# Window attention stage: token products over the whole array in three fp32r passes, staged in a ring and placed by transfers

## Chip, core and metric

The kernel runs on one core of one Trainium2 chip. TensorE (PE) does the matmuls, PEld is its weight load, VectorE is DVE, ScalarE is ACT, GpSimd is POOL, and SyncE (SP) issues every DMA of this kernel. The metric is the device time in microseconds (us) of one execution, the median of several.

## What is computed

Four residual blocks follow each other on x of 16 sequences x 256 tokens x 128 channels. The change lies in the last, which takes more than two thirds of the time. Cut to what matters:

```python
for i in range(6):                                   # DEPTH layers
    x = attn_layer(shift_tokens(x), Wqkv[i], ...) + x
    x = ffn_layer(shift_tokens(x), ...) + x
# attn_layer: 16 heads of 64, windows of 32 tokens; each looks at itself and the one before
q, k, v = split(x @ Wqkv)
q, k = l2norm(q) * qs, l2norm(k) * ksc, then rotary
attn = softmax(where(mask, -max, q @ k.T * 8))       # 32 x 64 per window and head
out = (attn @ v) in head order, then out @ Wo
```

The kernel never forms v. Since out @ Wo is a sum over heads of attn @ (x @ Wv_h @ Wo_h), it first makes one 128x128 matrix M_h = Wv_h Wo_h for each head (once in a layer) and then U_h = x @ M_h for each sequence. U is what this text calls the token products: 256 tokens x 16 heads x 128 channels.

## The kernel before, in words

The last stage (phase D) runs 6 layers x 16 sequences = 96 units, in 100 turns. Turn f works on several units at once: it projects q and k for unit f (chunks 0 to 4) and f-1 (chunks 5 to 7), takes the softmax of f-2 and makes its token products, runs attention for f-3 and the feed-forward of f-4. Each engine has an order written out by hand (the loops `for f in range(TURNS_D)`), and waits on semaphores. Nothing is reordered at run time, so an instruction that waits holds all behind it on its engine, SP's DMAs included.

Names. `project(n, i)` is 6 fp32r matmuls (a high and a low part of weights and tokens; three products of the parts) into bank 0 or 1; ACT squares the bank (`squares`), DVE multiplies it with the rotary table (`rotary_products`, L1428) into one of three slots `d_t`, and POOL adds halves (`rotary_sums`, L1815, into `d_rot`; `add_halves`, L1823). `norm_*`, `spread_norms` and `scale_keys` (L1464) apply the norms. `place_queries` (L2141) and `place_keys` (L2132) are 8 DMAs each on SP that bring `d_rot` into the layout of `d_q` and `d_k`; the first waits for POOL's eighth rotary sum, the second for DVE's second `scale_keys`. `scores` waits for both; so does POOL's first rotary sum of the next unit, which overwrites what `place_keys` reads. POOL's softmax steps are `scale_shifted` (L1832) and `softmax_scale` (L1838); ACT's is `softmax_exp` (L1676), DVE's are L1470, L1476, L1483 and the transposes L1496.

`token_products(n, w)` (L1957) makes U for window w of 8: plain fp32, and since a window has 32 tokens, four column groups of the array work side by side, one for each four heads. Its result has the 32 tokens of a window on 32 partitions and heads by groups of four down the 128, which is the layout in which `attention` reads `d_u`; ACT's `read_products` (L1684) copies each bank there. Windows use banks 5 and 4 in the order 5, 4, 5, 4, 5, 5, 4, 5; window w waits until an earlier one has left its bank. `attention(n, 0)` waits for the first windows' copies and `attention(n, 1)` for all. `head_matrices` makes the M_h in turn 16 l + 2 of layer l.

Of the kernel before, what the change touches and what calls it, by code (L numbers as in the profile page):

```python
# [67 lines left out]
LOADS_A, LOADS_B, LOADS_C, LOADS_CONST, CONSTS = 3, 4, 5, 10, 7  # L68
# [3 lines left out]
def build(nc, dram, out):  # L72
    ctx = ExitStack()
    with ctx:
# [14 lines left out]
        ones_row = sb("ones_row", [1, P])  # L89
# [5 lines left out]
        sel_r = sb("sel_r", [P, 4, 2, P], F32R)  # L95
        odd = sb("odd", [P, 1])
        z_split = sb("z_split", [P, 2, T], F32R)
        m_vo = sb("m_vo", [P, H, C])
        wvt = sb("wvt", [P, PAIRS, C])
        wo = sb("wo", [P, PAIRS, C])  # L100
        wqk_stage = sb("wqk_stage", [P, 2 * INNER])
        wqk_split = sb("wqk_split", [P, 8, 2, 2, P], F32R)
        x_split = sb("x_split", [P, 2, 2, T], F32R)
# [6 lines left out]
        ARENA = 30300  # L110
# [10 lines left out]
        parts_r = under_arena("parts_b", PARTS_B_AT, 2 * 4 * P * (1 + 2 * HB))  # L121
        WEIGHTS_C = 3 * PAIRS * C
        PARTS_C_AT = (4 * PAIRS + 1) * C + 3 * NT + TPS * C
        low_weights_c = under_arena("weights_c_low", C, WEIGHTS_C)
        parts_c = under_arena("parts_c", PARTS_C_AT, 4 * TPS * P + WEIGHTS_C)
# [529 lines left out]
        early = Local(1024, m_vo[:, :, :].rearrange("p h c -> p (h c)"))  # L655
# [12 lines left out]
        b_g = [lr(2, HB, UN), b_h]  # L668
        wb1_hi = x_split[:, :, :, :].rearrange("p a b c -> p (a b c)")
# [223 lines left out]
        ahead = Local(0, m_vo[:, :, :].rearrange("p h c -> p (h c)"))  # L893
        c_st, c_mv = ahead(NT, 6), ahead(NT, 2)
        d_st, d_mv = ahead(NT, 6), ahead(NT, 2)
        d_var, d_rstd, d_wn = ahead(NT), ahead(NT), ahead(NT)
        c_var, c_y, c_w = lc(NT), lc(NT), lc(NT)
        c_xn = lc(TPS, C)
        assert lc.at == PARTS_C_AT, lc.at
        lrc = Local(0, parts_c)  # L900
        c_xt, c_xt_lo = lrc(2, T), lrc(2, T)
# [4 lines left out]
        c_xf = lc(T)  # L906
# [262 lines left out]
        def phase_c_tensor(pe):  # L1169
# [86 lines left out]
            def sequence_turns(n, s, left):  # L1256
# [43 lines left out]
        d_xt = [ld(T) for _ in range(3)]  # L1300
# [12 lines left out]
        d_xf, d_v, d_r, d_wf, d_xc, d_xn = ld(T), ld(T), ld(T), ld(T), ld(T), ld(T)  # L1313
        d_gl = ld(2, T)
        d_h = ld(NF, T)
        tab_flat = tab[:, :, :, :, :].rearrange("p m k h t -> p (m k h t)")
# [5 lines left out]
         d_chain, d_act_chain, s_y2, s_xc, s_xn, s_up, s_gl, s_h, s_ffo, s_x_done, s_m, s_mvo, s_whi, s_wlo, s_tab,  # L1322
         loaded_qk, loaded_sc, loaded_vo, loaded_w1, loaded_w2) = (
# [4 lines left out]
                "chain act_chain y2 xc xn up gl h ffo x_done m mvo whi wlo tab "  # L1328
# [77 lines left out]
        def phase_d_vector(dve):  # L1406
# [161 lines left out]
            for v in (*d_xt, d_xf):  # L1568
                nc.vector.memset(v, 0.0).then_inc(s_zero, 1)
# [576 lines left out]
        def _(sp):  # L2146
# [230 lines left out]
```

## Time and profile before

| | us |
|---|---|
| median of 3 runs | 4245.19 (4243.02 to 4245.6) |
| profiled execution, its own time | 4247.19 |
| its span, first to last instruction | 4245.4 |
| PE busy in the span | 3898.6 (92%) |
| DVE busy | 3566.7 (84%) |
| ACT busy | 2619.0 (62%) |
| POOL busy | 2380.4 (56%) |
| DMA, mean share of the 16 engines | 23.4% |

The profiled execution stands 2.0 us above the median, and its span 0.2 us above. The page cuts the span into 40 slices of 106 us; phase D begins in slice 13. A share over the whole span mixes four phases with different limits, so phase D is read by its own windows and by one turn of the timeline. Times in the timeline are counted from the start of the span; a piece is printed as its start, its length, engine, line, operation, tiles and how many instructions it merges.

### The profile page before, as it was taken

How to read it: one execution, taken by the hardware profiler on the slowest of the kernel's cores; microseconds unless marked ns; L12 is line 12 of the kernel's file. 1: busy time of each engine (PE TensorE's matmuls, PEld its weight loads, DVE VectorE, ACT ScalarE, POOL GpSimd, SP SyncE). 2: the span in 40 equal slices, each digit the busy share in tenths (PEclk: the TensorE clock that was granted, in tenths of full speed). 3: DMA queues.
4: the chain of work that ended last, by engine and by line, in shares of the span. 5: the costliest groups of instructions: out<-in, count | busy, mean ns of one | idle time of the engine just before them, and what ended most of it. 6: DMA issues, size and time to landing. Idle time of an engine off the chain costs nothing.

```text
span 4245.4 us, 120089 instructions
## 1 busy us (share of the span) xinstructions
PE 3898.6 (92%) x48128; PEld 2739.2 (65%) x48128; DVE 3566.7 (84%) x5529; ACT 2619.0 (62%) x5518; POOL 2380.4 (56%) x2045
## 2 busy tenths in 40 slices
PE   3457998999995999999999999999999999999998
PEld 1225776777774676667766676667766676667675
DVE  7986556777776899989998899989998899989897
ACT  2442335666664666666667666666666666666665
POOL 0111001000002787878888788878878787878785
PEclk7668999999997999999999999999999999999999
DMA  3000000000001333233332333233332333333332
GB/s 104 0 0 1 1 1 1 1 0 0 0 1 40 71 95 81 64 80 88 79 76 67 77 90 81 68 76 88 79 77 66 75 92 81 69 76 70 93 75 68
DMA packets 264482, 238.94 MB, mean 56 GB/s; under 512 B 31524, under 2 KB 260136, under 8 KB 263208
## 3 DMA queue, kind: packets, MB, share of 16 engines
q1 hardware_dynamic: 263976, 231.82, 23.4%
q8 instruction: 363, 5.95, 0.6%
q14 instruction: 143, 1.17, 0.1%
HBM read 26.20 MB, written 4.19 MB: 7 GB/s over the span
## 4 chain that ended last, share of the span: by engine, by line
PE 72%; DVE 13%; ACT 7%; issue 3%; SPq 2%; POOL 1%; DMA 1%; DVEq 0%; ACTq 0%; POOLq 0%
PE bank L1957 14%; PE bank L1890 13%; PE bank L1975 8%; PE bank L1930 7%; PE bank L2017 5%; PE bank L834 4%; ACT arena L1109 3%; PE bank L2030 2%; PE bank L1923 2%; DVE arena L996 2%; PE bank L1901 2%; DVE arena L1006 2%; PE bank L1234 1%; PE bank L1225 1%; PE bank L1912 1%
## 5 line engine op out<-in xcount | busy, mean ns | idle before, releaser
L1428 DVE TENSOR_TENSOR arena<-bank,tab 128x1024 f32<-128x1024 f32 x768 | 936.5, 1220 | 187.5 <-ACT arena L1660 136.0
L1815 POOL TENSOR_TENSOR arena<-arena 128x512 f32<-128x512 f32 x768 | 1009.8, 1330 | 47.4 <-DMA arena<-arena 43.2
L1660 ACT ACTIVATE arena<-bank 128x512 f32<-128x512 f32 x768 | 458.1, 597 | 537.8 <-PE bank L1890 527.8
L1957 PE MATMUL bank<-m_vo,arena 128*32 128x512 f32 x6144 | 757.6, 599 | 17.3 <-DVE arena L1521 11.0
L1890 PE MATMUL bank<-x_split,wqk_split 128*128 128x256 f32 x4608 | 720.1, 299 | 35.0 <-DVE arena L1428 21.0
L1890 PEld LDWEIGHTS bank<-x_split,wqk_split 128*128 128x128 f32 x4608 | 605.1, 191 | 183.9 <-issue 94.3
L1823 POOL TENSOR_TENSOR arena<-arena 128x256 f32<-128x256 f32 x768 | 556.7, 736 | 162.4 <-ACT arena L1660 161.9
L1684 ACT ACTIVATE arena<-bank 128x512 f32<-128x512 f32 x768 | 456.4, 595 | 187.4 <-PE bank L1957 184.7
L1832 POOL TENSOR_TENSOR arena<-arena 128x1024 f32<-128x1024 f32 x192 | 371.6, 1936 | 261.0 <-DVE arena L1476 261.0
L1167 POOL TENSOR_TENSOR x_all<-x_all,arena 128x256 f32<-128x256 f32 x16 | 11.6, 726 | 833.8 <-DVE arena L988 833.8
L1838 POOL TENSOR_TENSOR arena<-arena 128x1024 f32<-128x1024 f32 x192 | 373.4, 1945 | 127.3 <-DVE arena L1489 127.0
L1930 PE MATMUL bank<-arena 128*32 128x128 f32 x12288 | 403.0, 273 | 0.6 <-issue 0.6
L1975 PE MATMUL bank<-arena 128*32 128x128 f32 x12288 | 373.7, 274 | 0.0
L1930 PEld LDWEIGHTS bank<-arena 128*32 128x32 f32 x12288 | 345.1, 110 | 37.5 <-issue 1.2
L1975 PEld LDWEIGHTS bank<-arena 128*32 128x32 f32 x12288 | 333.1, 110 | 31.4 <-issue 0.7
L1957 PEld LDWEIGHTS bank<-m_vo,arena 128*32 128x32 f32 x6144 | 159.3, 109 | 260.2 <-ACT arena L1684 140.3
L1109 ACT ACTIVATE arena<-bank,arena 128x256 f32<-128x256 f32 x512 | 235.4, 472 | 131.0 <-DVE arena L996 130.0
L2017 PE MATMUL bank<-arena,w 128*128 128x256 f32 (+1 forms) x1152 | 280.7, 380 | 2.4 <-ACT arena L1715 2.0
L1496 DVE STREAM_TRANSPOSE arena<-arena 128x1024 f32<-128x1024 f32 x192 | 235.0, 1224 | 25.8 <-POOL arena L1838 25.8
L1470 DVE TENSOR_REDUCE arena<-bank 128x16 f32<-128x1024 f32 x192 | 234.2, 1220 | 12.1 <-PE bank L1930 4.1
L1464 DVE TENSOR_TENSOR arena<-arena,bank 128x1024 f32<-128x1024 f32 x192 | 232.4, 1210 | 2.1 <-PE bank L1912 2.1
L1476 DVE TENSOR_TENSOR arena<-bank,arena 128x1024 f32<-128x1024 f32 x192 | 233.5, 1216 | 0.0
(252 smaller groups left out, 7159.8 us busy)
## 6 DMA issues: line engine op xcount, KB each, us to landing
arena<-arena SPq DMA_DIRECT2D x1536, 128.0 KB, 2.5
wqk_stage<-in_wqk SPq DMA_DIRECT2D x6, 1024.0 KB, 8.5
out_x<-x_all SPq DMA_DIRECT2D x7, 512.0 KB, 6.0
wvt<-in_wvt SPq DMA_DIRECT2D x6, 512.0 KB, 4.4
wo<-in_wo SPq DMA_DIRECT2D x6, 512.0 KB, 5.5
arena<-in_wbh SPq DMA_DIRECT2D x1, 2048.0 KB, 9.6
w<-in_w SPq DMA_DIRECT2D x6, 341.0 KB, 5.7
wqk_stage<-out_x SPq DMA_DIRECT2D x2, 512.0 KB, 4.8
```

The source lines that it names most:

```text
L1428: nc.vector.tensor_tensor(d_t[c % KS].rearrange("p k h t -> p k (h t)"), bank[c % 2][:, :].unsqueeze(1).to_broadcast([P, 2, 2 * T]), tab[: ...
L1660: nc.scalar.activation(d_sq[i % 4].rearrange("p h t -> p (h t)"), bank[c % 2][:, :], ACT.Square).then_inc(s_sq, 1)
L1684: nc.scalar.activation(d_u[:, 1 + w, :, :], bank[U_BANK[w]][:, :].rearrange("p (a c) -> p a c", a=QUADS), ACT.Copy).then_inc(s_uev, 1)
L1815: nc.gpsimd.tensor_tensor(d_rot[i // 4][:, i % 4, :, :], t[:, :, 0, :], t[:, :, 1, :], ALU.add).then_inc(s_ad, 1)
L1823: nc.gpsimd.tensor_tensor(sq[:, 0, :], sq[:, 0, :], sq[:, 1, :], ALU.add).then_inc(s_sa, 1)
L1832: nc.gpsimd.tensor_tensor(e, e, factor.to_broadcast([P, WPT, QUADS, 2 * WIN]), ALU.mult).then_inc(s_rm, 1)
L1838: nc.gpsimd.tensor_tensor(d_e[h], d_e[h], d_inv[h].unsqueeze(2).to_broadcast([P, 4 * QUADS, 2 * WIN]), ALU.mult)\
L1890: last = nc.tensor.matmul(bank[c % 2][:, h * T:(h + 1) * T], wqk_split[:, i, wp, h, :], x_split[:, n % 2, xp, :], start=(q == 0), stop=(q ...
L1930: last = nc.tensor.matmul(bank[2 + b][g * WIN:(g + 1) * WIN, (2 * v + a) * P:(2 * v + a + 1) * P], d_q[:, a, g, at:at + WIN], d_k[:, a, g, ...
L1957: last = nc.tensor.matmul(bank[U_BANK[w]][g * WIN:(g + 1) * WIN, :], d_xt[n % 3][:, w * WIN:(w + 1) * WIN], m_vo[:, 4 * g:4 * g + 4, :].re ...
L1975: last = nc.tensor.matmul(bank[6][v * WIN:(v + 1) * WIN, h * C:(h + 1) * C], d_pt[h][:, at, :], d_u[:, WPT * h + v + z, r, :], start=(r == ...
L2017: last = nc.tensor.matmul(bank[UP_BANK[c]][0:m, half * T:(half + 1) * T], w1_of(n)[:, first + c * P:first + c * P + m], d_xn, start=True, ...
```

## The change

Token products take pairs of windows now: index t of `w // 2, w % 2` names a head group g and a token half t, and one product covers 128 tokens x 4 heads on the whole array. It is three fp32r matmuls (high x high, high x low, low x high) of 128x128 weights (the tokens) and 512 columns. The tokens' parts are the `x_split` that the projections use, which has three slots now; the M_h get parts too (`m_split`), the high by ACT, the low by a new DVE step.

A result has 128 tokens on 128 partitions, so it isn't in `d_u`'s layout. ACT copies it to `u_stage`, a ring of two head groups, and SP brings each group to `d_u` by four DMAs (`place_products`), 16 for a unit. A group waits for its two copies and for the attention of the unit before. ACT waits before it reuses a slot, and `attention` waits, for both halves, until all 16 transfers landed. `attention(f - 3, 0)` moved behind `project(f - 1, 6)` and `ffn_up(f - 4, 2)`. `d_xt` has one slot instead of three. The weights of M_h are loaded into `wqk_stage`, after the projection weights were taken from it. The kept input comes back in four fetches over two slots, two of them later. `normalise` takes two sequences a turn in turns 0 to 6 (seven, then six, in turns 0 and 1 before). Some tiles of phases B and C moved into the new tiles.

```diff
@@ token_products(n, w), TensorE
-                for g in range(4):
-                    last = nc.tensor.matmul(bank[U_BANK[w]][g * WIN:(g + 1) * WIN, :], d_xt[n % 3][:, w * WIN:(w + 1) * WIN],
-                                            m_vo[:, 4 * g:4 * g + 4, :].rearrange("p a c -> p (a c)"), start=True, stop=True,
-                                            tile_position=(0, g * WIN))
+                g, t = w // TPS, w % TPS
+                for q, (xp, mp) in enumerate(((0, 0), (0, 1), (1, 0))):
+                    last = nc.tensor.matmul(bank[U_BANK[w]][:, :], x_split[:, n % 3, xp, t * P:(t + 1) * P],
+                                            m_split[:, mp, 4 * g:4 * g + 4, :].rearrange("p a c -> p (a c)"),
+                                            start=(q == 0), stop=(q == 2))
@@ attention(n, h), TensorE
-                pe.wait_ge(s_uev, NW * n + 4 * h + 4)
+                pe.wait_ge(s_ud[0], 128 * (n + 1))
+                pe.wait_ge(s_ud[1], 128 * (n + 1))
@@ read_products(n, *windows), ScalarE
-                    at_least(act, s_at, 2 * n - 1 if w < 3 else 2 * n)
-                    nc.scalar.activation(d_u[:, 1 + w, :, :], bank[U_BANK[w]][:, :].rearrange("p (a c) -> p a c", a=QUADS),
-                                         ACT.Copy).then_inc(s_uev, 1)
+                    g, t = w // TPS, w % TPS
+                    at_least(act, s_ud[g % 2], 128 * n + 64 * (g // 2))
+                    nc.scalar.activation(u_stage[:, g % 2, t, :], bank[U_BANK[w]][:, :], ACT.Copy).then_inc(s_uev, 1)
@@ new, VectorE, once in a layer
+            def head_matrices(l):
+
+                for g in range(4):
+                    dve.wait_ge(s_mvo, 4 * l + g + 1)
...
+                    nc.vector.tensor_tensor(lo, src, hi.bitcast(F32), ALU.subtract).then_inc(s_mlo, 1)
@@ new, SP
+        def place_products(sp, n, *groups):
+
+            if not here(n):
+                return
+            for g in groups:
+                sp.wait_ge(s_uev, NW * n + TPS * (g + 1))
+                at_least(sp, s_at, 2 * n)
+                for w in range(WPT):
+                    sp.dma_start(d_u[g * WIN:(g + 1) * WIN, 1 + w:2 + w + WPT:WPT, :, :].rearrange("p t r c -> p t (r c)"),
+                                 u_stage[w * WIN:(w + 1) * WIN, g % 2, :, :]).then_inc(s_ud[g % 2], 16)
@@ the loop of SP
                 place_queries(sp, n)
+                place_products(sp, n - 1, 0, 1)
                 place_keys(sp, n)
+                place_products(sp, n - 1, 2, 3)
+                if n % SEQS == 0 and n > 0:
+                    load_vo(sp, layer_of(n))
@@ the loop of TensorE
                 project(f - 1, 5)
-                attention(f - 3, 0)
                 project(f - 1, 6)
                 ffn_up(f - 4, 2)
+                attention(f - 3, 0)
                 project(f - 1, 7)
```

SP, one turn in mid phase D of the kernel before: the queries (L2141), then the keys (L2132), each transfer 32 partitions x 4 x 256 values.

```order
L2141 DMA arena<-arena 32x4x256 [waits d_s,d_ad]
L2141 DMA arena<-arena 32x4x256 x7
L2132 DMA arena<-arena 32x4x256 [waits d_s,d_mR]
L2132 DMA arena<-arena 32x4x256 x7
```

The same turn of the changed kernel; queries are L2168, keys L2159 and products L2149.

```order
L2168 DMA arena<-arena 32x4x256 [waits d_s,d_ad]
L2168 DMA arena<-arena 32x4x256 x7
L2149 DMA arena<-u_stage 32x2x512 [waits d_at,d_uev]
L2149 DMA arena<-u_stage 32x2x512 x3
L2149 DMA arena<-u_stage 32x2x512 [waits d_at,d_uev]
L2149 DMA arena<-u_stage 32x2x512 x3
L2159 DMA arena<-arena 32x4x256 [waits d_s,d_mR]
L2159 DMA arena<-arena 32x4x256 x7
L2149 DMA arena<-u_stage 32x2x512 [waits d_at,d_uev]
L2149 DMA arena<-u_stage 32x2x512 x3
L2149 DMA arena<-u_stage 32x2x512 [waits d_at,d_uev]
L2149 DMA arena<-u_stage 32x2x512 x3
```

Eight transfers stand between the queries and the keys now, and eight behind the keys: 32 in a turn instead of 16.

TensorE, the first half of a turn before, from the chunk 5 projection (L1890) to chunk 7; L1975 is attention, L2017 the third up projection.

```order
L1890 MATMUL bank<-x_split,wqk_split 128x256 [waits d_rp,d_wlo,d_split]
L1890 MATMUL bank<-x_split,wqk_split 128x256 x5
L1975 MATMUL bank<-arena 32x128 [waits d_xt,d_uev,d_pt]
L1975 MATMUL bank<-arena 32x128 x31
L1890 MATMUL bank<-x_split,wqk_split 128x256 [waits d_rp,d_wlo,d_split]
L1890 MATMUL bank<-x_split,wqk_split 128x256 x5
L2017 MATMUL bank<-arena,w 85x256 [waits d_h]
L2017 MATMUL bank<-arena,w 85x256
L1890 MATMUL bank<-x_split,wqk_split 128x256 [waits d_rp,d_wlo,d_split]
L1890 MATMUL bank<-x_split,wqk_split 128x256 x5
```

The same place of the changed kernel, where L1900 is the projection, L1987 attention and L2029 the up projection.

```order
L1900 MATMUL bank<-x_split,wqk_split 128x256 [waits d_rp,d_wlo,d_split]
L1900 MATMUL bank<-x_split,wqk_split 128x256 x5
L1900 MATMUL bank<-x_split,wqk_split 128x256 [waits d_rp,d_wlo,d_split]
L1900 MATMUL bank<-x_split,wqk_split 128x256 x5
L2029 MATMUL bank<-arena,w 85x256 [waits d_h]
L2029 MATMUL bank<-arena,w 85x256
L1987 MATMUL bank<-arena 32x128 [waits d_ud1,d_xt,d_ud0,d_pt]
L1987 MATMUL bank<-arena 32x128 x31
L1900 MATMUL bank<-x_split,wqk_split 128x256 [waits d_rp,d_wlo,d_split]
L1900 MATMUL bank<-x_split,wqk_split 128x256 x5
```

Attention stands behind chunk 6 and the up projection, and waits for the landings (`d_ud0`, `d_ud1`) instead of the copies (`d_uev`).

## Rows read from the trace of the kernel before

**Rows 1.** Windows of phase D: window, length, busy of each engine, PEclk, DMA share, GB/s

```profile
2000.00:2400.00 400.00, 394.14 (x5978) 279.25 (x5970) 363.63 (x441) 270.75 (x513) 324.39 (x279) 1.00 0.31 71
```

**Rows 2.** Timeline of TensorE: token products inside one turn, and the next turn's first

```profile
2517.03 1.03 PE L1957 MATMUL bank<-m_vo,arena 128*32 128x512 f32 x8
2517.99 1.69 PE L1890 MATMUL bank<-x_split,wqk_split 128*128 128x256 f32 x12
2519.61 1.92 PE L1957 MATMUL bank<-m_vo,arena 128*32 128x512 f32 x16
2521.47 0.44 PE L1986 MATMUL bank<-ident,x_all 128*128 128x128 f32 x2
...
2546.24 1.03 PE L1957 MATMUL bank<-m_vo,arena 128*32 128x512 f32 x8
```

**Rows 3.** Timeline of TensorE in phase C: three fp32r passes of 512 columns

```profile
1016.01 0.72 PE L1194 MATMUL bank<-parts_c 128*128 128x512 f32 x2
1016.57 0.39 PE L1194 MATMUL bank<-weights_c_low,parts_c 128*128 128x512 f32 x1
1016.80 1.03 PE L1214 MATMUL bank<-ident,arena 128*128 128x128 f32 x8
```

**Rows 4.** Timeline of SP's DMA issues: queries L2141 and keys L2132

```profile
2520.21 5.12 SPq L2141 DMA_DIRECT2D arena<-arena  x8
2525.80 5.10 SPq L2132 DMA_DIRECT2D arena<-arena  x8
2549.40 5.13 SPq L2141 DMA_DIRECT2D arena<-arena  x8
```

**Rows 5.** The lines of the keys' transfers, and of the first loads, for issue and landing

```profile
L2132 SPq DMA_DIRECT2D arena<-arena x768: 585/603/2277, 1363.6 to 4198.5; - x192
...
DMA to landing us min/median/max: 2.4/2.5/4.2
...
L2115 SPq DMA_DIRECT2D cols_d<-in_cols_d x6: 432/432/711, 37.1 to 3403.7; - x6
```

**Rows 6.** Timeline of DVE: the second scale_keys, softmax sum, then rotary products 3 and 4

```profile
2524.57 1.21 DVE L1464 TENSOR_TENSOR arena<-arena,bank 128x1024 f32<-128x1024 f32 x1
...
2534.37 1.23 DVE L1428 TENSOR_TENSOR arena<-bank,tab 128x1024 f32<-128x1024 f32 x1 [0.16 <-POOL arena L1815]
2535.86 0.48 DVE L1529 SCALAR_TENSOR_TENSOR arena<-bank,cols_d,arena 128x256 f32<-128x256 f32 x1 [0.27 <-ACT arena L1723]
2536.26 1.21 DVE L1428 TENSOR_TENSOR arena<-bank,tab 128x1024 f32<-128x1024 f32 x1
```

**Rows 7.** Timeline of POOL from the last softmax step to the eighth rotary sum

```profile
2531.03 1.90 POOL L1838 TENSOR_TENSOR arena<-arena 128x1024 f32<-128x1024 f32 x1 [0.25 <-DVE arena L1489]
2532.99 2.51 POOL L1815 TENSOR_TENSOR arena<-arena 128x512 f32<-128x512 f32 x2
...
2541.07 0.74 POOL L1823 TENSOR_TENSOR arena<-arena 128x256 f32<-128x256 f32 x1 [0.46 <-ACT arena L1660]
2542.65 0.73 POOL L1823 TENSOR_TENSOR arena<-arena 128x256 f32<-128x256 f32 x1 [0.83 <-ACT arena L1660]
...
2546.47 2.91 POOL L1815 TENSOR_TENSOR arena<-arena 128x512 f32<-128x512 f32 x2
```

**Rows 8.** Timeline of ACT: the copy of window 4

```profile
2525.18 0.59 ACT L1684 ACTIVATE arena<-bank 128x512 f32<-128x512 f32 x1
```

**Rows 9.** Timeline of TensorE: chunk 5, attention, chunk 6, up projection, chunk 7

```profile
2536.60 0.97 PE L1890 MATMUL bank<-x_split,wqk_split 128*128 128x256 f32 x6
2537.50 1.96 PE L1975 MATMUL bank<-arena 128*32 128x128 f32 x64
2539.39 0.98 PE L1890 MATMUL bank<-x_split,wqk_split 128*128 128x256 f32 x6
2540.20 1.03 PE L2017 MATMUL bank<-arena,w 128*85 128x256 f32 x4
2540.88 1.06 PE L1890 MATMUL bank<-x_split,wqk_split 128*128 128x256 f32 x6
```

**Rows 10.** Timeline of SP: the fetch of the kept input, late in the last layer

```profile
3950.57 5.13 SPq L2141 DMA_DIRECT2D arena<-arena  x8
3956.17 5.60 SPq L2132 DMA_DIRECT2D arena<-arena  x8
3961.88 1.25 SPq L2187 DMA_DIRECT2D wqk_stage<-out_x  x2
...
3984.63 5.12 SPq L2141 DMA_DIRECT2D arena<-arena  x8
```

More of the change, by code:

```diff
@@ L905, in build @@
         lc.at += lrc.at
-        c_xf = lc(T)
+        c_xn, c_xf = ahead(TPS, C), ahead(T)
         c_qk = [lc(PAIRS, 2, T) for _ in range(2)]
@@ L1299, in build @@
         KS = 3
-        d_xt = [ld(T) for _ in range(3)]
+        d_xt = ld(T)
         d_sq = [ld(2, T) for _ in range(4)]
@@ L1415, in split_low_tokens @@
                 dve.wait_ge(s_xh, n + 1)
[L1416 removed]
+                nc.vector.tensor_tensor(x_split[:, n % 3, 1, :], d_xt, x_split[:, n % 3, 0, :].bitcast(F32), ALU.subtract)\
                     .then_inc(s_split, 1)
+            def head_matrices(l):
+                for g in range(4):
+                    dve.wait_ge(s_mvo, 4 * l + g + 1)
+                    hi, lo = (m_split[:, part, :, :].rearrange("p (b j odd) c -> p b odd j c", b=2, odd=2)[:, g // 2, g % 2] for part in range(2))
+                    src = bank[5 - g % 2][:, :].rearrange("p (j c) -> p j c", j=4)
+                    nc.vector.tensor_tensor(lo, src, hi.bitcast(F32), ALU.subtract).then_inc(s_mlo, 1)
             def rotary_products(n, *chunks):
@@ L1594, in phase_d_vector @@
                 ffn_gate(f - 4, 2)
+                if here(f - 2) and (f - 2) % SEQS == 0:
+                    head_matrices(layer_of(f - 2))
                 norm_weight(f - 1)
@@ L1616, in phase_d_vector @@
                 turn_probabilities(f - 2, 0)
-                if f < 2:
-                    normalise(*range(3 + 7 * f, min(10 + 7 * f, SEQS)))
+                if f < 7:
+                    normalise(*range(3 + 2 * f, min(5 + 2 * f, SEQS)))
                 done = f - 4 - SEQS * (LAYERS - 1)
@@ L1889, in project @@
                         for q, (wp, xp) in enumerate(((0, 0), (0, 1), (1, 0))):
-                            last = nc.tensor.matmul(bank[c % 2][:, h * T:(h + 1) * T], wqk_split[:, i, wp, h, :], x_split[:, n % 2, xp, :],
+                            last = nc.tensor.matmul(bank[c % 2][:, h * T:(h + 1) * T], wqk_split[:, i, wp, h, :], x_split[:, n % 3, xp, :],
                                                     start=(q == 0), stop=(q == 2))
@@ L1911, in spread_norms @@
                 for b in range(2):
-                    last = nc.tensor.matmul(bank[7][:, b * T:(b + 1) * T], sel_r[:, 2 * h + b, 0, :], d_z, start=True, stop=True)
+                    last = nc.tensor.matmul(bank[7][:, b * T:(b + 1) * T], sel_r[:, 2 * h + b, :], d_z, start=True, stop=True)
                 last.then_inc(s_R, 1)
@@ L2184, in _ @@
                     sp.wait_ge(kept, 16 * (NT // KEEP))
-                    for g in range(NT // KEEP):
-                        s = slice(g * KEEP, (g + 1) * KEEP)
-                        sp.dma_start(x_kept[g], out[s].rearrange("n p c -> p n c")).then_inc(back[g], 16)
+                    fetch_kept(sp, 0)
+                    fetch_kept(sp, 1)
+                if n == LAST - 4:
+                    sp.wait_ge(s_normed, SEQS + 1)
+                    fetch_kept(sp, 2)
+                if n == LAST:
+                    sp.wait_ge(s_normed, SEQS + 2)
+                    fetch_kept(sp, 3)
                 if n % SEQS == 4 and layer_of(n) + 1 < LAYERS:
-                    load_vo(sp, layer_of(n) + 1)
                     load_qk(sp, layer_of(n) + 1)
```

115 lines of the change are left out of this document (59 added, 56 removed).

## The prediction

> **What bounds the kernel now.** I read phase D by windows first. In 400 us of it PE is busy 394 at a granted clock of 1.00, its upper level of 2.4 GHz; DVE is busy 364 (91%), POOL 324, ACT 271 [rows 1]. That says PE is the bound and that a cheaper PE step can win little before DVE is next: DVE's floor is 0.91 of the turn. The turn is read from one line that recurs: the first token products at 2517.03 and 2546.24 are 29.2 us apart [rows 2], the queries' transfers at 2520.21 and 2549.40 are 29.19 apart [rows 4].
>
> Then I looked for another loop of the same length, since a full engine can hide one. There is one, through SP and POOL. Call Q the start of the queries' transfers, 2520.21. They take SP 5.12 us, to 2525.33. The keys' transfers start at 2525.80, right when DVE's second scale_keys ends (2524.57 + 1.21 = 2525.78) [rows 4, 6]. SP had 0.5 us of slack there. Eight issues take 5.10 us, a step of 0.64; one occupies SP for 0.603 (median) and lands 2.5 after its start [rows 5]. So the last starts at 2530.30 and lands at 2532.80. POOL's first rotary sum needs that landing, and POOL's softmax_scale ends at 2531.03 + 1.90 = 2532.93; it starts at 2532.99 [rows 7]. Its eighth ends at 2546.47 + 2.91 = 2549.38, and the queries start at 2549.40. The loop is 12.78 (Q to the first sum) + 16.41 (first sum to the next Q) = 29.19. So PE and this loop tie, and what lengthens the loop costs its full length.
>
> **What the change takes off PE.** A window takes 0.96 us alone (2517.03 to 2517.99) and a pair 1.86 (2519.61 to 2521.47) [rows 2]; two lone windows and three pairs in a turn make 7.5. The new form stands in phase C: three fp32r passes of 512 columns from 1016.01 to the next work at 1016.80, 0.79 alone, with 0.23 a pass once it runs (1016.57 to 1016.80) [rows 3]. A pair is then 0.79 + 3 x 0.23 = 1.48; the turn 2 x 0.79 + 3 x 1.48 = 6.0. PE saves 1.5 us a turn, 140 us over 96 units, if PE alone set the turn. It doesn't, by the loop above.
>
> **What it adds to SP.** 16 transfers a turn, as large as the old (32 partitions x 4 KB). Their issue cost is not in the trace. Nearest are the queries and keys with a step of 0.64; plain loads cost 0.43, 0.47 with the gap [rows 5]. The new ones have half as many, twice as long runs. I take 0.60, nearest to the same size and kind, and keep 0.47 and, should the DMA engines hold SP up, 0.75 (an estimate; the keys' longest single issue was 2.28). Eight of them stand between queries and keys: 5.16 + 8 x 0.60 = 9.96, so the keys start at Q+9.96, while scale_keys had them ready at Q+5.57. The last key lands 4.50 + 2.5 later, at Q+16.95.
>
> **What it adds to ACT.** The ring holds two head groups. The copy of window 4 may start only when group 0 has landed, and that is issued behind the queries: Q+5.16, its fourth issue 1.80 later, landing 2.5 later, Q+9.46. Before, that copy started at 2525.18, Q+4.97 [rows 8]. Behind it in ACT's order stand squares 2 and 3, the feed-forward's rsqrt and the second softmax_exp, and on that wait DVE's second sum, its reciprocal and POOL's last softmax_scale, which ended at 2532.93 [rows 7]: 7.75 after the copy's start. These steps follow one another without a gap that would absorb the shift, so the first rotary sum can't start before Q+9.46+7.75 = Q+17.2. The two paths meet within 0.3; the later counts: **Q+17.2 instead of Q+12.78, 4.4 us later.**
>
> **From the first sum to the next Q.** These 16.41 us hold 15.1 of POOL work, waits of 0.46 and 0.83 for ACT's squares of chunks 6 and 7, and some drag [rows 7]. Does the new PE order shorten them? Chunk 6 waits until DVE has emptied its bank (rotary product 4, 2536.26 + 1.21 = 2537.47), and product 3 before it waits for POOL's first sum (the 0.16 in the row) [rows 6]; so chunk 6 can't move ahead of that sum plus 4.5. From 2537.50 PE now does chunk 6 (0.81), the up projection (0.68), attention (1.89), and chunk 7 starts at 2540.88, exactly where it started before [rows 9]. The wait for chunk 7's squares stays, the one for chunk 6's is refilled by it. 16.4 stays. Attention would start 6.0 after the first sum. Its last products are issued behind the keys: Q+9.96+5.14+7 x 0.60+2.5 = Q+21.8, which is 4.6 after the first sum. So this new wait is covered by 1.4 us; beyond that it costs PE, and the loop, one for one.
>
> **The sum.** Turn 17.2 + 16.4 = 33.6 instead of 29.19, +4.4. There are 95 intervals between the 96 query groups: 95 x 4.4 = 418. PE's 1.5 goes into its idle time and is worth nothing. Every transfer behind the keys (8 products) ends about Q+20 and SP is free until Q+33.6, so M_h's loads cost nothing, though the queue takes them later. The kept input is fetched behind the products now: 3961.88 was 5.7 after the keys' start at 3956.17, and that turn already lasts 34.1 (3950.57 to 3984.63) instead of 29.2; the eight products (4.8 us) and the later keys are in front of it now, about +5 [rows 10]. DVE's four subtractions per layer (some 0.6 us each) and the layer changes' extra POOL and ACT work fall as much on the loop as before; I put them at nothing, with 10 us either way. normalise's spread and the tiles of phases B and C change no work: nothing. 4247.2 + 418 + 5 = 4670 for the profiled execution; it was 2.0 above the median, so 4668.
>
> The bounds of that case: issues at 0.47 give Q+16.8 by the ring, a turn of 33.2, +380 in all: 4630. At 0.75, Q+18.1 by the queue, +5.4: 4760.
>
> A rule of the Trainium skill speaks on SP's part. The rows show an issue of 0.60 against a landing of 2.5, and eight in a row cost 5.1 of SP [rows 4, 5]. "DMA: Bandwidth & Descriptors", section "Issuing engines are not separate DMA queues", says that issuing from more engines only saves the sequencer's time to initiate a DMA, "which is usually small relative to the DMA itself". Taken so, 16 more issues would be nearly free and PE's saving would show (about 4100 to 4250); by the rows they stand in the loop in full, which gives 4668.
>
> **Rivals.** (1) *Faster: issues are hidden, DVE or PE sets the turn.* It decides if the eight products cost SP less than its slack of 0.5 us and the ring no more than PE saves. Then the turn falls toward 28.0: 95 x -1.2 = -115, 4130. Against it: the slack is in the rows and the cheapest issue there, 0.43, makes 3.5 for eight. (2) *The loop lengthens by less.* POOL's 16.4 holds 1.3 of waits; if ACT, less crowded relative to PE, gives chunks 6 and 7 sooner, it goes to 15.1 and the turn to 32.3: +3.1 x 95, 4540. If the ring's chain also closes up and issues cost 0.47, the queue sets Q+15.9, the turn is 31.0: 4420. For it: I laid only the paths I found. Against: DVE's product 4 pins chunk 6. (3) *Dearer: twice the traffic.* If landings slow as well as issues, by 1 us each, the queue, the ring and the cover of attention's wait go together: 4770 and more. Against: landings stayed at 2.5 median in the present bursts. (4) *The change doesn't do what it says*, the passes no faster than the plain fp32 form. It gives the forecast too, as PE isn't the bound any more, and needs no chance of its own.
>
> **Chances.** Forecast (4620 to 4700) 0.57; less by rival 2 0.22, most of it in 4530 to 4620; dearer, 4700 to 4770, 0.10, beyond 0.05; faster, rival 1, 0.05; within 0.2% 0.01 (about what a measurement of this kernel can tell from no change, here 8 us). The range 4530 to 4770 leaves out about 0.18. Slower 0.94.
>
> **What would show it.** In the profile after: queries' transfers 33 to 34 us apart; SP busy with issues for about 20 us a turn without a gap from Q to Q+20; the keys starting right behind the eighth product, not on scale_keys; ACT waiting about 4 us for a DMA at one copy in eight (window 4); POOL's first rotary sum waiting for a DMA or ending the softmax; PE busy near 83% in phase D, waiting at scores for the keys, and products of 0.75 us a window. If the queries come 29 us apart or less, the loop was not what I took it for. If attention's first matmul waits for DMAs, the cover of 1.4 us was wrong. If PE's clock falls in its new gaps, the turn grows beyond this; the rows have no gap as long, so I can't price it.

## The result and the profile after

The changed kernel takes 4836.59 us (median of 4 runs, 4835.45 to 4842.1), the kernel before beside it 4245.4 us (median of 4): ratio 1.139, 95% interval 1.138 to 1.141. It is slower, as forecast, but by 591 us instead of 423: outside the range of 4530 to 4770. Its profiled execution has a span of 4840.3 us.

The page: the busy line, the granted clock in 40 slices, one line of the chain that ended last, and three groups (busy, mean ns | idle before, releaser). L1436 is `rotary_products`, L1696 the copies to the ring, L1968 the token products.

```profile
PE 3987.5 (82%) x44288; PEld 3089.4 (64%) x44288; DVE 3588.7 (74%) x5550; ACT 2638.1 (55%) x5518; POOL 2378.1 (49%) x2045
...
PEclk7769999999979999999899999999989999999899
...
POOL 26%; SPq 24%; PE 16%; DVE 11%; issue 10%; ACT 7%; DMA 6%; DVEq 0%; ACTq 0%; POOLq 0%
...
L1436 DVE TENSOR_TENSOR arena<-bank,tab 128x1024 f32<-128x1024 f32 x768 | 937.0, 1220 | 620.4 <-ACT arena L1671 554.5
...
L1696 ACT ACTIVATE u_stage<-bank 128x512 f32<-128x512 f32 x768 | 458.0, 597 | 729.2 <-DMA arena<-u_stage 467.7
L1968 PE MATMUL bank<-m_split,x_split 128*128 128x512 f32 x2304 | 756.9, 456 | 27.1 <-ACT u_stage L1696 8.9
```

The engines' busy sums hardly moved; the span grew around them. POOL and SP's issues make up half of the chain, where PE made up 72% before (the page of the kernel before, the same line):

```profile
PE 72%; DVE 13%; ACT 7%; issue 3%; SPq 2%; POOL 1%; DMA 1%; DVEq 0%; ACTq 0%; POOLq 0%
```

And the products' busy time is 756.9 us, 7.9 a turn, though their form was meant to take less.

SP's timeline in one turn (queries L2168, products L2149, keys L2159), where rows 4 has queries and keys alone:

```profile
2570.72 5.18 SPq L2168 DMA_DIRECT2D arena<-arena  x8
2576.00 5.10 SPq L2149 DMA_DIRECT2D arena<-u_stage  x8
2581.20 5.11 SPq L2159 DMA_DIRECT2D arena<-arena  x8
2586.47 6.22 SPq L2149 DMA_DIRECT2D arena<-u_stage  x8
```

Four bursts without a gap. The keys start 10.5 us after the queries, on the heels of the products. Then ACT's copy of window 4, POOL's first rotary sum, its wait for ACT's squares of chunk 7, its seventh and eighth sums, DVE's rotary products 3 and 4 around the gate (L1537), and chunk 4's projection behind its gap, each from its engine's timeline:

```profile
2580.42 0.60 ACT L1696 ACTIVATE u_stage<-bank 128x512 f32<-128x512 f32 x1 [5.05 <-DMA arena<-u_stage]
```

```profile
2588.37 2.51 POOL L1825 TENSOR_TENSOR arena<-arena 128x512 f32<-128x512 f32 x2 [0.37 <-DMA arena<-arena]
...
2599.11 0.73 POOL L1833 TENSOR_TENSOR arena<-arena 128x256 f32<-128x256 f32 x1 [2.01 <-ACT arena L1671]
...
2602.93 2.94 POOL L1825 TENSOR_TENSOR arena<-arena 128x512 f32<-128x512 f32 x2
```

```profile
2589.75 1.23 DVE L1436 TENSOR_TENSOR arena<-bank,tab 128x1024 f32<-128x1024 f32 x1 [0.47 <-POOL arena L1825]
2592.03 0.48 DVE L1537 SCALAR_TENSOR_TENSOR arena<-bank,cols_d,arena 128x256 f32<-128x256 f32 x1 [1.06 <-ACT arena L1734]
2592.43 1.22 DVE L1436 TENSOR_TENSOR arena<-bank,tab 128x1024 f32<-128x1024 f32 x1
```

```profile
2582.91 1.62 PE L1900 MATMUL bank<-x_split,wqk_split 128*128 128x256 f32 x6 [4.76 <-DVE arena L1436]
```

From Q (2570.72) the copy waits 5.05 us for a landing and starts at Q+9.70, the first sum at Q+17.65, the eighth sum ends 17.50 after the first began. The next queries start at 2605.89, so the turn is 35.17.

What had no counterpart before is PE's clock. Windows inside that turn (window, length, busy by engine, granted clock, DMA share, GB/s):

```profile
2570.00:2577.00 7.00, 6.51 (x39) 5.19 (x38) 7.00 (x7) 4.03 (x9) 4.03 (x4) 1.00 0.63 144
2577.00:2583.00 6.00, 1.24 (x12) 1.08 (x10) 1.46 (x2) 2.52 (x6) 1.41 (x2) 0.76 0.91 201
2583.00:2589.00 6.00, 6.00 (x27) 4.03 (x28) 5.46 (x10) 3.79 (x7) 4.52 (x3) 0.67 0.85 196
2589.00:2604.00 15.00, 14.93 (x317) 12.37 (x316) 12.49 (x15) 8.94 (x16) 12.61 (x12) 1.00 0.31 71
```

PE idles 4.76 us before chunk 4; the clock falls to the lower level (1.2 GHz) for part of the next two windows, with PE fully busy again in the second. Chunk 4's six matmuls take 1.62 us instead of 0.95 to 1.06 [rows 9].

One turn is one sample, so the table below takes, from the starts in the timelines, all turns. Q, keys' start K, copy of window 4 and first sum X are medians over 76 of them (units 4 to 79), "turn" is the mean over all 95 intervals.

| us | Q to K | Q to copy 4 | Q to X | X to next Q | turn, mean |
|---|---|---|---|---|---|
| before | 5.60 | 4.97 | 13.47 | 15.94 | 29.81 |
| after | 10.44 | 9.72 | 18.30 | 17.21 | 35.97 |

6.16 a turn over 95 intervals is 585 of the 595 us by which the spans differ. The rest is start and end.

### The profile page after: what moved, and what is told of

It is laid out like the page before. It is cut to its first block, busy times and chain, and to the rows that moved or that the text cites. A ratio compares the mean times of both kernels' runs of the same rounds, so it can differ in the third digit from the quotient of the medians.

```text
span 4840.3 us, 114439 instructions
## 1 busy us (share of the span) xinstructions
PE 3987.5 (82%) x44288; PEld 3089.4 (64%) x44288; DVE 3588.7 (74%) x5550; ACT 2638.1 (55%) x5518; POOL 2378.1 (49%) x2045
## 3 DMA queue, kind: packets, MB, share of 16 engines
q14 instruction: 158, 1.29, 0.1%
## 4 chain that ended last, share of the span: by engine, by line
POOL 26%; SPq 24%; PE 16%; DVE 11%; issue 10%; ACT 7%; DMA 6%; DVEq 0%; ACTq 0%; POOLq 0%
POOL arena L1825 17%; SPq L2168 8%; SPq L2149 8%; SPq L2159 7%; POOL arena L1833 5%; DMA arena<-arena 4%; PE bank L834 4%; POOL arena L1842 4%; ACT arena L1107 3%; DVE arena L994 2%; DVE arena L1004 1%; PE bank L1232 1%; PE bank L1223 1%; DMA arena<-u_stage 1%; PE bank L1968 1%
## 5 line engine op out<-in xcount | busy, mean ns | idle before, releaser
L1436 DVE TENSOR_TENSOR arena<-bank,tab 128x1024 f32<-128x1024 f32 x768 | 937.0, 1220 | 620.4 <-ACT arena L1671 554.5
L1900 PE MATMUL bank<-x_split,wqk_split 128*128 128x256 f32 x4608 | 761.0, 312 | 474.4 <-DVE arena L1436 467.9
L1900 PEld LDWEIGHTS bank<-x_split,wqk_split 128*128 128x128 f32 x4608 | 658.3, 207 | 560.7 <-issue 542.9
L1696 ACT ACTIVATE u_stage<-bank 128x512 f32<-128x512 f32 x768 | 458.0, 597 | 729.2 <-DMA arena<-u_stage 467.7
L1968 PE MATMUL bank<-m_split,x_split 128*128 128x512 f32 x2304 | 756.9, 456 | 27.1 <-ACT u_stage L1696 8.9
L1671 ACT ACTIVATE arena<-bank 128x512 f32<-128x512 f32 x768 | 447.8, 597 | 573.6 <-PE bank L1900 562.7
L1968 PEld LDWEIGHTS bank<-m_split,x_split 128*128 128x128 f32 x2304 | 459.7, 221 | 218.0 <-ACT u_stage L1696 119.3
L1987 PE MATMUL bank<-arena 128*32 128x128 f32 x12288 | 374.4, 274 | 7.7 <-issue 4.3
L1987 PEld LDWEIGHTS bank<-arena 128*32 128x32 f32 x12288 | 334.1, 110 | 61.8 <-issue 44.0
L2029 PE MATMUL bank<-arena,w 128*128 128x256 f32 (+1 forms) x1152 | 285.9, 384 | 3.7 <-ACT arena L1726 2.0
```

The source lines that it names most:

```text
L1436: nc.vector.tensor_tensor(d_t[c % KS].rearrange("p k h t -> p k (h t)"), bank[c % 2][:, :].unsqueeze(1).to_broadcast([P, 2, 2 * T]), tab[: ...
L1671: nc.scalar.activation(d_sq[i % 4].rearrange("p h t -> p (h t)"), bank[c % 2][:, :], ACT.Square).then_inc(s_sq, 1)
L1696: nc.scalar.activation(u_stage[:, g % 2, t, :], bank[U_BANK[w]][:, :], ACT.Copy).then_inc(s_uev, 1)
L1900: last = nc.tensor.matmul(bank[c % 2][:, h * T:(h + 1) * T], wqk_split[:, i, wp, h, :], x_split[:, n % 3, xp, :], start=(q == 0), stop=(q ...
L1968: last = nc.tensor.matmul(bank[U_BANK[w]][:, :], x_split[:, n % 3, xp, t * P:(t + 1) * P], m_split[:, mp, 4 * g:4 * g + 4, :].rearrange("p ...
L1987: last = nc.tensor.matmul(bank[6][v * WIN:(v + 1) * WIN, h * C:(h + 1) * C], d_pt[h][:, at, :], d_u[:, WPT * h + v + z, r, :], start=(r == ...
```

## The experiments

In each experiment one theory stands against rivals, named by letters. Theory A: the time is lost in the placements, by SP's order (eight issues ahead of the keys) and the ring. Rivals: the fp32r form and its clock (B), the ring alone, the traffic.

**Without the placements.**

```diff
@@ from the changed kernel; SP's place_products calls are left out
-                    at_least(act, s_ud[g % 2], 128 * n + 64 * (g // 2))
-                    nc.scalar.activation(u_stage[:, g % 2, t, :], bank[U_BANK[w]][:, :], ACT.Copy).then_inc(s_uev, 1)
+                    at_least(act, s_at, 2 * n - 1 if w < 3 else 2 * n)
+                    nc.scalar.activation(d_u[:, 1 + w, :, :], bank[U_BANK[w]][:, :].rearrange("p (a c) -> p a c", a=QUADS),
+                                         ACT.Copy).then_inc(s_uev, 1)
@@ attention
-                pe.wait_ge(s_ud[0], 128 * (n + 1))
-                pe.wait_ge(s_ud[1], 128 * (n + 1))
+                pe.wait_ge(s_uev, NW * n + 4 * h + 4)
```

> The changed kernel without its placements: ACT copies each token product straight into d_u with the waits of the kernel before, attention waits for copies, SP issues only queries and keys. Left out: the 16 transfers of a unit, so the products lie in d_u in the wrong order and the output is not the reference's; every other instruction is kept. Theory A (the loss is all in the placements: eight more issues between queries and keys, and the ring): the queries' transfers come 28.3 to 29.2 us apart and the time is 4160 to 4250, since PE saves 1.5 us a turn but the loop through SP and POOL of 29.2 stays. Rival B (the fp32r form itself, its three-slot split, or a lower PE clock costs the time): the turn stays above 30 and the time above 4320.

Measured 4277.18 us, 1.007 of before (1.005 to 1.009). The placements cost 559 of the 591 us, and B falls: PE's form costs little. But A's numbers were missed as well (time at most 4250, turn at most 29.2; the median turn is 29.64). The products, cheaper by 1 us a turn here, gained nothing in this order of PE, and it is 31 us slower than before. The run with attention's old order, below, shows why.

```profile
L1968 PE MATMUL bank<-m_split,x_split 128*128 128x512 f32 x2304 | 661.8, 410 | 30.9 <-DVE arena L1529 12.1
```

661.8 against 757.6 before for the same products: 6.9 us a turn for 7.9. The prediction had 6.0 for 7.5.

**The queue's share alone.**

```diff
@@ from the run without placements, with place_products called as in the changed kernel
+                at_least(sp, s_ud[g % 2], 128 * n + 64 * (g // 2))
...
-                    sp.dma_start(d_u[g * WIN:(g + 1) * WIN, 1 + w:2 + w + WPT:WPT, :, :].rearrange("p t r c -> p t (r c)"),
-                                 u_stage[w * WIN:(w + 1) * WIN, g % 2, :, :]).then_inc(s_ud[g % 2], 16)
+                    sp.dma_start(u_stage[w * WIN:(w + 1) * WIN, :, g % 2, :],
+                                 base[g * WIN:(g + 1) * WIN, :, :].rearrange("p (a b) t -> p a (b t)", a=2)).then_inc(s_ud[g % 2], 16)
```

> As the run without placements (copies straight into d_u, attention waits for copies; the output is not the reference's), but SP issues 16 transfers of the same size and run length at the same places of its queue, with the same waits for the copies, from a constant tile into the unused stage; nobody on another engine waits for them. This has the queue's share and no ring. Theory A1 (the queue's place between queries and keys is enough): keys start 10.4 to 10.5 us after the queries, POOL's first rotary sum 17.0 to 17.7 after them, turn 33.4 to 35, time 4650 to 4800. Rival A2 (the ring, ACT's wait for landings, is what lengthens the turn; the queue would be hidden without it): turn under 31, time under 4420.

4799.3 us, 1.130 (1.127 to 1.134). The added wait is SP's own, for an earlier idle transfer into the same slot, and the products still start 5.23 after the queries (5.22 in the changed kernel). No engine uses what is moved, and 522 us are back. The wait appears elsewhere; all three lines are of the waits of this kernel between 2000 and 4000 us (sum, times, longest):

```profile
POOL arena L1825 <- DMA arena<-arena: 318.3, 57, 7.2
PEld bank L1933 <- DMA arena<-arena: 267.2, 57, 6.2
PE bank L1933 <- DMA arena<-arena: 244.4, 56, 5.8
```

POOL's first sum waits 5.6 us a turn for the keys' landing (318.3 / 57), and the scores wait with it. Rival A2 falls: without a ring the first sum starts at Q+18.46 (median), no earlier than in the changed kernel.

**The same transfers behind the keys.**

```diff
-                place_products(sp, n - 1, 0, 1)
                 place_keys(sp, n)
-                place_products(sp, n - 1, 2, 3)
+                place_products(sp, n - 1, 0, 1, 2, 3)
```

> The run with the queue's share alone (copies straight into d_u, 16 transfers of a unit from a constant tile that nobody else waits for; the output is not the reference's), with one move: all 16 stand behind the keys. Same number of transfers, same traffic. Theory A1 (what costs is the place in SP's order, between queries and keys): keys start about 5.4 us after the queries again, turn near that of the run without transfers, 29.6 to 30.4 (it was 35.3 median with eight in between), time 4275 to 4350. Rival F (32 transfers a turn cost through the traffic, wherever they stand): turn over 32, time over 4450.

4320.78 us, 1.018 (1.015 to 1.021). As many transfers, as much traffic, 479 us less. SP's timeline of one turn (L2168 queries, L2159 keys, L2149 the 16), and this kernel's DMA share over 2000 us, which is higher than the changed kernel's 0.55:

```profile
2509.74 5.10 SPq L2168 DMA_DIRECT2D arena<-arena  x8
2515.18 5.93 SPq L2159 DMA_DIRECT2D arena<-arena  x8
2521.22 11.68 SPq L2149 DMA_DIRECT2D u_stage<-base  x16
2539.46 5.11 SPq L2168 DMA_DIRECT2D arena<-arena  x8
```

```profile
2000.00:4000.00 2000.00, 1875.73 (x26162) 1521.98 (x26164) 1776.67 (x2178) 1333.86 (x2507) 1575.91 (x1345) 0.99 0.63 144
```

This is the sharpest pair: place, not amount. Traffic (F) costs at most the 44 us over the run without placements. An ordinary turn shows none of them: the median turn is 29.63, against 29.64 without the transfers. Of the 40.9 us by which the 95 intervals differ in sum, 39.4 stand in six turns, one at each change of layer (behind units 17, 33, 49, 65 and 81) and the one of the fetch (87), in which SP has other loads in its order too.

**The real transfers behind the keys.** The same edit of SP's loop in the complete changed kernel.

> The changed kernel, complete, with SP's order changed alone: queries, keys, then all 16 product transfers. The queue's cost between queries and keys is gone; group 0 lands later. Theory L (ring and queue are two paths of about equal length, so that taking one away shows the other, and moving the products back lengthens the ring): keys start 5.5 us after the queries, the copy of window 4 starts 15.1 to 15.4 after them (9.7 in the changed kernel), POOL's first sum 23.3 to 23.7 after, turn 40 to 41, time 5230 to 5340. Rival M (the ring costs nothing of its own, only keys behind products do): turn 29.6 to 31, time 4320 to 4420.

5368.98 us, 1.265 (1.262 to 1.267). The keys start at Q+5.44 (median), the copy of window 4 at Q+15.22, the first sum at Q+22.80, turn 41.0 median. L holds in its mechanism, and for the keys, the copy and the turn. Two of its numbers missed: the first sum came 0.5 earlier than its range, and the total 29 us above it (X to next Q is 18.05). M falls. ACT's line:

```profile
2525.37 0.60 ACT L1696 ACTIVATE u_stage<-bank 128x512 f32<-128x512 f32 x1 [10.39 <-DMA arena<-u_stage]
```

So the ring is a second path of about the queue's length. In the changed kernel the keys' landing ends last: the first sum starts 0.13 after it (median), and 0.40 after the end of the softmax, the end of the ring's chain. Here it is the ring: the keys landed 10.2 before the first sum. Neither order tested is good with 16 issues of 0.64 us: ahead of the keys they delay the keys, behind them the ring. Not tested were other splits around the keys, and products issued by another engine than SP.

**PE's gap filled.**

```diff
+                pe.wait_ge(s_sub, 2 * n + 2)
+                for i in range(20):
+                    nc.tensor.matmul(bank[2][:, :], ident_bf[:, :], mask_bf[:, 1, :, :].rearrange("p a k -> p (a k)"), start=True, stop=True)
...
+                fill_gap(f - 2)
                 project(f, 4)
```

> The changed kernel with 20 bf16 matmuls of 512 columns (about 4.3 us at the upper clock) in TensorE's order ahead of chunk 4's projection, where it idles about 4.8 us in a turn; they go to a score bank that is free by then and is overwritten later. Theory C (PE's clock falls to 1.2 GHz behind that gap and the slow chunk 4, products and sums hand 1.1 to 2 us a turn on to ACT, DVE and POOL): granted clock back to 1.00 in phase D, turn 34.0 to 34.6 instead of 35.2 to 36.2, time 4660 to 4760. Rival D (the clock's fall costs nothing, since SP's queue and the ring end last anyway): time 4830 to 4850, or slower by the filler.

4810.74 us, 26 less than the changed kernel, where C expected 77 to 177 and a turn of at most 34.6 (the mean is 35.66). D's number was missed too, from the other side. C's first half held (the clock column):

```profile
2000.00:2400.00 400.00, 371.89 (x4652) 280.62 (x4654) 305.59 (x376) 226.48 (x423) 266.60 (x226) 1.00 0.56 128
```

The clock stays at its upper level and X to next Q falls from 17.21 to 16.54 (medians), 0.67. But Q to X rose from 18.30 to 18.70: this execution has 117 product issues of over 0.8 us instead of 62. Whether the filler caused that is open; the run shows no link. The clock's loss is worth 0.3 (the mean turn's change) to 0.7 us a turn. That is small for a stretch in which chunk 4 alone took 0.6 us longer and the token products behind it ran partly at the lower level; the first sum, which comes next, waits for the keys' landing and not for PE.

Where the 0.67 comes from shows in ACT's copy of window 5, which waits for a token product. First the changed kernel, then the filled one, each in the turn whose copy of window 4 waited 5 us for a landing:

```profile
2585.84 0.60 ACT L1696 ACTIVATE u_stage<-bank 128x512 f32<-128x512 f32 x1 [1.73 <-PE bank L1968]
```

```profile
2576.70 0.60 ACT L1696 ACTIVATE u_stage<-bank 128x512 f32<-128x512 f32 x1 [0.47 <-PE bank L1968]
```

Behind these copies ACT has the gelu that DVE's gate (L1537) waits for. Over the turns, the gate waits 0.72 us in the changed kernel (median) and nothing in the filled one, though its ring is no earlier (copy 4 at Q+10.67). Product 4 starts 3.73 and 2.92 after the first sum, against 2.91 before.

The Trainium skill ("TensorE: Matmul & The Clock Gate", section "Part 1: The HAM clock gate") says that the clock follows how busy PE has recently been. The trace agrees: it fell with a gap of 4.76 us and stayed up when the gap was filled.

**The order of attention undone.**

```diff
+                attention(f - 3, 0)
                 project(f - 1, 6)
                 ffn_up(f - 4, 2)
-                attention(f - 3, 0)
```

> The changed kernel with one thing undone: the first half of attention stands before chunk 6's projection again, as in the kernel before. It then waits for the last products' landing, about 6.1 us after POOL's first rotary sum, with chunk 6 and 7 behind it. Theory A: chunk 7 starts about 0.5 us later, turn +0.3 to +0.7, time 4865 to 4910. Rival E (the move costs or gains nothing, chunk 7 is held by DVE's rotary product): time within 10 us of 4837.

In the changed kernel: 4936.37 us, 1.163 (1.153 to 1.172), from two executions 32 us apart. X to next Q is 18.28 instead of 17.21, the mean turn 36.81 instead of 35.97. The price is 0.8 to 1.1 a turn, more than the 0.3 to 0.7 expected, and E falls.

The same edit in the run without placements:

> The run without placements (copies straight into d_u; the output is not the reference's), and the first half of attention ahead of chunk 6's projection again, as in the kernel before. Without placements the chain through the turn went from DVE's rotary product 4 to chunk 6, up projection, attention, chunk 7. Theory G (the moved attention stands in that chain, and hides the fp32r form's saving): chunk 7 starts 0.8 to 1.2 us earlier, turn median 28.4 to 29.0 instead of 29.6, time 4170 to 4230, below the kernel before. Rival H (the chain through keys and POOL holds the turn at 29 whatever PE does): 4260 to 4285 as without the move.

4226.8 us, 0.996 (0.994 to 0.998), X to next Q 15.69 instead of 16.37. G holds, at the upper edge of its range, and H falls. PE's timeline of the two, without the move and with it; L1986 is attention, L2028 the up projection, L1900 chunks 5, 6, 7:

```profile
2524.81 0.95 PE L1900 MATMUL bank<-x_split,wqk_split 128*128 128x256 f32 x6
2525.69 1.95 PE L1986 MATMUL bank<-arena 128*32 128x128 f32 x64
2527.58 0.98 PE L1900 MATMUL bank<-x_split,wqk_split 128*128 128x256 f32 x6
2528.40 1.02 PE L2028 MATMUL bank<-arena,w 128*85 128x256 f32 x4
2529.07 1.06 PE L1900 MATMUL bank<-x_split,wqk_split 128*128 128x256 f32 x6
```

```profile
2512.70 0.95 PE L1900 MATMUL bank<-x_split,wqk_split 128*128 128x256 f32 x6
2514.23 0.95 PE L1900 MATMUL bank<-x_split,wqk_split 128*128 128x256 f32 x6 [0.57 <-DVE arena L1436]
2515.01 1.03 PE L2028 MATMUL bank<-arena,w 128*85 128x256 f32 x4
2515.97 1.96 PE L1986 MATMUL bank<-arena 128*32 128x128 f32 x64
2517.85 0.98 PE L1900 MATMUL bank<-x_split,wqk_split 128*128 128x256 f32 x6
```

From chunk 5 to chunk 7: 4.26 and 5.15. Attention fills the wait for DVE's rotary product 4 in the first; in the second PE waits, and attention stands in front of chunk 7. The move repairs part of what the placements break, and costs 50 us where they are absent. In the old order the new form of the products is worth 19 us.

**A version without placements that is complete.** Each window is multiplied on its own 32 columns of the array, as before the change, by parts in bf16.

```diff
+                for q, (xp, mp) in enumerate(((0, 0), (0, 1), (1, 0))):
+                    for g in range(4):
+                        last = nc.tensor.matmul(bank[U_BANK[w]][g * WIN:(g + 1) * WIN, :], x_bf[:, n % 3, xp, w * WIN:(w + 1) * WIN],
+                                                m_bf[:, mp, 4 * g:4 * g + 4, :].rearrange("p a c -> p (a c)"),
+                                                start=(q == 0), stop=(q == 2), skip_group_check=True, tile_position=(0, g * WIN))
...
+                nc.vector.tensor_tensor(x_bf[:, n % 3, 1, :], d_xt, x_bf[:, n % 3, 0, :], ALU.subtract).then_inc(s_xb, 1)
```

> A version that needs no placements: token products by windows on four column groups, as in the kernel before, with the high and low parts in bf16 (three products), so that the result lies in d_u's layout and ACT copies it straight there; attention in the old order. It adds one ACT copy and one DVE subtraction of 128x256 a turn for the bf16 parts of the tokens. If theory G holds: a window takes 0.65 to 0.75 us of PE instead of 0.92, turn 28.7 to 29.3, time 4180 to 4245. Rival (the added ACT and DVE steps of 0.4 to 1.3 us go into the chain through keys and POOL): turn 29.6 to 30.5, time 4270 to 4350. The bf16 parts carry fewer bits than fp32r's.

4272.6 us, 1.006 (1.004 to 1.008): the rival's range, though the median turn, 29.16, lies in G's. DVE's new step takes long (its line; min/median/max ns):

```profile
L1427 DVE TENSOR_TENSOR x_bf<-arena,x_bf x96: 412/1711/2032, 1335.9 to 4196.7; 128x256 bf16<-128x256 f32 x96
```

Moved ahead of the second `softmax_shift`, where POOL idles:

> The bf16 version with DVE's subtraction of the tokens' low bf16 part moved from the end of a turn to just ahead of the second softmax_shift, where POOL stands idle for 2.1 us. At the end of a turn the step took 1.71 us, ending 0.27 us after POOL's softmax_scale beside it ended; the same shape takes 0.4 us from PSUM. Theory J (a DVE step with both inputs in SBUF stands still while POOL works): it takes 0.35 to 0.6 us at the new place, turn median 28.7 to 29.0 instead of 29.16, time 4215 to 4245, at or below the kernel before (4245.6). Rival K (the step is long by its types, or the loop takes the 0.4 us where it now stands): 1.3 us or more a step, or time 4255 to 4280.

```profile
L1427 DVE TENSOR_TENSOR x_bf<-arena,x_bf x96: 414/416/598, 1333.5 to 4166.4; 128x256 bf16<-128x256 f32 x96
```

J holds for the step, 1711 to 416 ns, and not for the rest: its turn (29.31 median, 28.7 to 29.0 expected) and time were missed. The time, 4253.34 us, is 1.0017 of before (1.0007 to 1.0027): 19 us better than at the old place, and still no gain. The products take 606.0 us of PE instead of 757.6, 1.6 less a turn, but PE is not alone at the bound. No complete version tried here beats the kernel before.

**The fetch.** `if n == LAST - 8` became `LAST - 10`.

> The changed kernel with the first two fetches of the kept input issued two units earlier in SP's order. Theory: the turn that lasts 46.4 us in the changed kernel (34.1 before), where DVE waits 9.5 us for the fetch, becomes an ordinary one of 35 to 36: time 4837 - 10 = 4827 (4820 to 4833). Rival (the wait is only moved to another turn): 4833 to 4842.

4827.82 us (4822.84 to 4832.81), 9 less, with the long turn gone. The ranges of the two kernels don't overlap, but it is two runs.

The means of all turns in one table:

| kernel | turn, mean | time | what the step adds to the turn |
|---|---|---|---|
| before | 29.81 | 4245 | |
| without placements, attention in the old order | 29.64 | 4227 | fp32r form, -0.17 |
| without placements | 30.17 | 4277 | moved attention, +0.53 |
| queue alone | 35.61 | 4799 | eight issues ahead of the keys, +5.44 |
| changed kernel | 35.97 | 4837 | the ring and attention's wait for landings, +0.36 |

## Why the prediction was wrong

**What bounds the kernel: right.** A second loop of PE's length through SP, the keys' landing and POOL. The idle transfers show it: nothing but SP's work was added, and the turn grew by 5.4 with eight of the 16 ahead of the keys, by 0.4 with all behind them.

**PE's saving worth nothing: right here, its size wrong.** 1.0 us a turn at the upper clock instead of 1.5. Phase C's pass of 0.23 us was read inside one group of three; with pairs and bank waits it was 410 ns a matmul and 6.9 us a turn. In the changed kernel even that is eaten by the lower clock. Without placements and in attention's old order it is worth 19 us.

**The queue: right in mechanism, mis-sized.** I took a step of 0.60. The products' issues cost what the keys' cost, 0.65 (5.10 for eight), so K is Q+10.44 instead of Q+9.96. Q to X grew by 4.83 instead of 4.4, and that is K's own growth (4.84). Single issues of over 0.8 us, half of them between 1.36 and 1.80, are 90 of 3072 here and 38 of 1536 before. Each one ahead of the keys' landing lengthens its turn, but they add nothing to the growth: the mean of Q to X grew by 4.73, no more than the median.

**The ring: right in place and size** (copy 4 at Q+9.72, forecast 9.46), and right that it meets the queue: without it the first sum is no earlier (18.46). The sum took the ring as the later of the two by 0.25; measured, the queue's landing ends last and the ring's chain 0.27 before it.

**"16.4 stays" is the step that failed.** The stretch from the first sum to the next queries grew by 1.27 (15.94 to 17.21, medians), nearly all of it in one wait of POOL, the one for ACT's squares of chunk 7: 0.82 before, 2.01 after (in the rows shown 0.83 [rows 7] and 2.01). The prediction let chunk 7 start "exactly where it started before"; it starts 8.74 after the first sum instead of 7.41. Medians of the same turns, in us:

| run | first sum to next queries | first sum to chunk 7 | POOL's wait for its squares |
|---|---|---|---|
| before | 15.94 | 7.41 | 0.82 |
| without placements, attention in the old order | 15.69 | 7.13 | 0.59 |
| without placements | 16.37 | 7.90 | 1.29 |
| changed kernel, gap filled | 16.54 | 8.10 | 1.47 |
| changed kernel | 17.21 | 8.74 | 2.01 |

The runs split the 1.27 in three:

- 0.43 is there without any placement (16.37), and moving attention back takes it away and more (15.69). It comes from the new order of PE. PE waits for product 4 before chunk 6, and the 1.9 us of attention then stand between chunk 6 and chunk 7 instead of in that wait. I had laid chunk 6, the up projection and attention without a gap from the end of product 4, as if the old start of chunk 7 left room for that.
- 0.67 is the clock: it comes back when the gap is filled (16.54), with the wait of DVE's gate for the gelu. I had pinned chunk 6 to product 4 and held product 4 fixed. I had named the clock among what would make the prediction wrong, and left it without a price, while the sum itself opened a gap of over 4 us in PE before chunk 4. The filled run also has its first sum 0.4 later, so not all of the 0.67 need be the clock's.
- 0.17, from 16.37 to 16.54, remains for the ring and the landings that attention waits for. No run separates them.

The ring alone doesn't make the gate wait: with the gap filled the gate waits for nothing (median). In the queue's run, which has no ring, it doesn't wait either, but there the clock falls elsewhere, behind the first sum (0.52 from 2498 to 2504, the first sum being at 2497.95). The order of PE wasn't neutral either way: with placements the move is worth 0.8 to 1.1 us, without them it costs 0.5.

**The cover of attention's wait: too large.** Forecast 1.4 us. The last products land 6.12 after the first sum (forecast 4.6), attention starts at 6.86 (forecast 6.0): 0.7 was left, and it sufficed.

**One turn as a base.** 12.78 and 16.41 were one turn's; the medians are 13.47 and 15.94. The sums are near each other (29.19 and 29.41), but the split differs by 0.5 to 0.7.

**The rest.** The mean turn: 6.16 forecast as 4.4; 0.43 of the gap is Q to X, 1.27 the other half, together 1.7 of 1.76 (the halves are medians, the turn a mean). Over 95 intervals 585 us were measured and 423 forecast, the fetch included: 162 of the 169 us by which 4668 missed. The rest is start and end. The fetch was right: the turn went from 34.1 to 46.4 us, 6 more than its neighbours' growth, forecast 5. Rival 1 and the reading by which 16 more issues are nearly free (4100 to 4250) fall with the queue's run. Rival 2 (less) was given 0.22 and is refuted; rival 3 (dearer) was the right side, but by its own mechanism not: landings stayed at 2.4 and 2.5 us median. The range's upper end held no price for the clock or the new order of PE.

## What to carry to other kernels

A transfer placed in an in-order queue costs its issue time to all that stand behind it, and nothing where nobody waits for those: count the issues between a ready value and its user, before looking at bandwidth. When an engine is full, look for a second loop of the same length, and price a change in both. When a sum opens a gap of several microseconds in TensorE, price its clock and whoever feeds the next step there too. Before work is moved on a full engine, look which wait it used to fill.

## What was not expected of the hardware

- A 128x256 subtraction on DVE with both inputs in SBUF took 1711 ns (median) beside POOL's softmax_scale and 416 ns where POOL was idle. The changed kernel's own L1416, of the same shape and beside POOL's work, takes 1.35 us (median). With one input in PSUM the shape takes 0.40 us beside POOL too (the changed kernel's L1511 at 2603.91). The Trainium skill ("SBUF — State Buffer", section "Who interferes with whom") says that a DVE instruction with two SBUF inputs contends with a GpSimd instruction that reads SBUF, while one with at most one SBUF input, outside the 2-port modes, doesn't. The Trainium skill states further, on the same page in section "Summary: rules for kernel authors", that of two that contend the second to issue waits until the first ends. All three durations agree, and so does the move's effect.
- Most issues of SP take 0.60 us; those of over 0.8 us, most of them 1.0 to 2.1, are 2 or 3 in 100 in the kernel before and the changed one (38 of 1536, 90 of 3072) and up to 7 (200 of 3072 with the idle transfers behind the keys). What makes an issue long wasn't found.
- 16 more transfers of 128 KB a turn, with a DMA share of 0.63, left the landing at 2.4 to 2.5 us (median) and cost 44 us in all, nearly none of it in ordinary turns (29.63 against 29.64, medians).
